# A three-stage transformer block: the last attention chunk's closing steps moved into the first steps of the second feed-forward

## The chip, the cores and the metric

The kernel runs on one core of one Trainium2 chip. The metric is the device time of one execution in microseconds (us), as the median of several runs. TensorE (PE) does matmuls and its own weight loads, VectorE (DVE), ScalarE (ACT) and GpSimd (POOL) work elementwise, and SyncE (SP) issues most DMAs. Each engine takes its own instructions in order and waits on semaphores.

## The reference

The input x has 8 sequences of 512 rows of 256 numbers, 4096 rows in all. Three stages follow one another, and each needs the whole output of the one before only through its own rows, except for the ranking of the rows by expert:

```
x = x + 0.5 * ffn(layernorm(x))
x = x + attention(layernorm(x))
x = x + 0.5 * ffn(layernorm(x))

def attention(x):                       # 16 heads of 16, causal, per sequence of 512
    q, k, v = x @ Wq.T, x @ Wk.T, x @ Wv.T
    out = softmax(mask(q k.T / 4)) @ v
    return out @ Wo.T

def ffn(x):                             # both feed-forwards have the same weights
    shared = (silu(x @ w1) * (x @ w2)) @ w3             # 1024 hidden
    scores = sigmoid(x @ router_w)                      # 16 experts
    top2 = the two largest of scores + bias
    routed = sum over the top2 e of scores[e] * swiglu_e(x)   # 256 hidden each
    return shared + routed
```

All is float32. The large products are made of three products of a high and a low part (a value and its rest after rounding), summed in PSUM.

## The kernel before

The program is a row of blocks, each of which ends when every engine has come to its end: a first norm, the first feed-forward (tiles named `f_`, the same function as the second), the attention (`at_`), and the second feed-forward (`f_` too). In the function `feed_forward` the second one is the case `exact`.

**The attention** works on 8 chunks c of 512 rows (a chunk is one sequence) and on 4 groups of 4 heads in each, so on 32 groups G; `TG` is 32. All engines run the same double loop, over rounds i and over 11 steps s of a round, and small tables say what stands at which (i, s). Round i makes the scores of group i+1 (`score1`, for the row maxima) and of group i (`score2`, then the exponentials on ACT), and at step 8 the product of group i-1 with the values (`weigh`, L2258). The groups of a chunk are followed, some rounds later, by its closing: the sums are turned over (`turn_over`, L2087), stored and fetched back broadcast over partitions (`send` L1807, `fetch` L1814), the product is scaled (L2092), multiplied with Wo (`project_out`, L2282), added to x (L2101), normed (L2039, L2045, POOL L1884 and L1886, L2128), turned (`turn2`, L2292 on PE, L2013 on ACT) and multiplied with the router weights (`route`, L2303, `logits` L2107). In rounds 32 to 37 there is no group left, and only the closing of chunks 6 and 7 is done. `shift` (L2065) negates a group's maxima; SP lays them down with L1789, and the group's `score2` waits for that DMA.

**The second feed-forward** has three parts. The shared part runs over 5 of 8 chunks and 8 slices j of the hidden size, 40 steps n = 8c + j (`BEHIND` is 5): PE multiplies slice n with w1 and w2 (`up`, L1408, 12 matmuls), then slice n-1 with w3 (`down`, L1424 and L1428, 12 matmuls). ACT makes silu (L1034) and the high part (L1038), DVE the product `f_hid` (L1250) and the low part (L1266). At j = 2 and 3 the next chunk's x is split (L984, L1087), at j = 0 the last chunk's result is added to x (L1213). Ahead of the first step the shared weights w1, w2, w3 are loaded in six pieces of 512 KB (SP L687) and split: high parts by ACT (L991), low parts of two by DVE (L1333) and of four by POOL (L916). The routing stands in the same steps: `routing(n)` on DVE finds the two best experts of all 4096 rows and the slot of each in a list sorted by expert, done in `slots` at n = 9 (L1149 to L1151); then POOL sends each row to its two slots in `rows_by_slot` with 64 indirect DMAs (`send`, L931), after loading rows in 16 pieces of 256 KB into four buffers (`load`, L922). From `INVERT_AT` = 13 on, eight times at every second step, DVE marks (`marks`) and PE inverts the list, which `homes` reads at n = 31. SP meanwhile loads the high parts of the 16 experts' weights, 768 KB each (`load_high`, L700), the last two after `homes`.

The routed part then runs over 80 blocks of 128 sorted rows. Its first block is fetched by SP (`fetch`, L735) when all 64 indirect DMAs have landed, and turned on PE (L1472) between `up` and `down` of the last shared step. Its weights' low parts come through a ring (L725). The last part does the remaining three chunks of the shared part and the sums.

## Time and profile before

| what | value |
|---|---|
| median of 3 runs | 1559.57 us (1558.65 to 1566.25) |
| the profiled execution's own time | 1568.19 us |
| its span, first to last instruction | 1566.0 us |
| mean granted TensorE clock | 0.968 of full |
| PE busy | 1466.1 us, 94% of the span |
| DVE, ACT, POOL busy | 960.9, 662.3, 594.4 us |

Times of rows count from the span's start. A row of the timeline has the start, the busy time, the engine and line, the operation with its tiles, how many instructions are merged (x), and in brackets how long the engine had been idle and what released it. The three runs differ by 7.6 us among themselves.

### The profile page before, as it was taken

How to read it: one execution, taken by the hardware profiler on the slowest of the kernel's cores; microseconds unless marked ns; L12 is line 12 of the kernel's file. 1: busy time of each engine (PE TensorE's matmuls, PEld its weight loads, DVE VectorE, ACT ScalarE, POOL GpSimd, SP SyncE). 2: the span in 40 equal slices, each digit the busy share in tenths (PEclk: the TensorE clock that was granted, in tenths of full speed). 3: DMA queues.
4: the chain of work that ended last, by engine and by line, in shares of the span. 5: the costliest groups of instructions: out<-in, count | busy, mean ns of one | idle time of the engine just before them, and what ended most of it. 6: DMA issues, size and time to landing. Idle time of an engine off the chain costs nothing. (4 is left out here: it accounts for less than half of the span.)

```text
span 1566.0 us, 29057 instructions
## 1 busy us (share of the span) xinstructions
PE 1466.1 (94%) x8999; PEld 1195.1 (76%) x9032; DVE 960.9 (61%) x2015; ACT 662.3 (42%) x1338; POOL 594.4 (38%) x836
## 2 busy tenths in 40 slices
PE   4999999999989979999999999948999999999998
PEld 4888888888878766667766666537888888888887
DVE  4678855555545657677677666316774455565566
ACT  2334444343433535665665566514322333443332
POOL 4618830233323023464466444403487033333100
PEclk9999999999999989999999999858999999999999
DMA  9696989535385953354555454224396344347841
GB/s 316 249 365 227 347 318 353 190 107 183 106 293 169 333 150 93 90 130 117 141 135 128 118 127 121 80 96 144 129 343 227 111 145 127 123 153 249 284 143 54
DMA packets 176804, 286.32 MB, mean 183 GB/s; under 512 B 20754, under 2 KB 125714, under 8 KB 176418
## 3 DMA queue, kind: packets, MB, share of 16 engines
q1 hardware_dynamic: 134914, 206.83, 41.8%
q0 software_dynamic: 19104, 56.64, 9.8%
q10 hardware_dynamic: 22656, 21.11, 4.6%
q8 instruction: 81, 1.33, 0.3%
q14 instruction: 49, 0.40, 0.1%
HBM read 144.20 MB, written 110.36 MB: 163 GB/s over the span
## 5 line engine op out<-in xcount | busy, mean ns | idle before, releaser
L1408 PE MATMUL f_bank<-f_xparts,f_sw 128*128 128x512 f32 x1536 | 382.0, 398 | 12.4 <-DVE f_sw L1333 9.2
L1408 PEld LDWEIGHTS f_bank<-f_xparts,f_sw 128*128 128x128 f32 x1536 | 287.3, 193 | 69.0 <-issue 12.2
L963 POOL DMA_INDIRECT outputs_by_choice<-f_yr,f_home x160 | 153.4, 959 | 394.5 <-DVE f_yr L1359 338.4
L2056 DVE TENSOR_REDUCE at_mx<-at_ps 128x1 f32<-128x384 f32 (+3 forms) x352 | 213.9, 632 | 111.9 <-PE at_ps L2188 104.7
L1963 ACT ACTIVATE at_pT<-at_ps 128x512 f32<-128x512 f32 (+1 forms) x352 | 194.4, 559 | 71.6 <-PE at_ps L2204 62.7
L1879 POOL TENSOR_SCALAR_AFFINE_SELECT at_pT<-at_pT 128x128 f32<-128x128 f32 (+2 forms) x352 | 124.2, 361 | 221.1 <-ACT at_pT L1963 216.7
L931 POOL DMA_INDIRECT rows_by_slot<-f_xq,slot x128 | 145.2, 1134 | 111.5 <-DVEq L1152 73.2
L1250 DVE TENSOR_TENSOR f_hid<-f_sil,f_bank 128x512 f32<-128x512 f32 x128 | 87.9, 687 | 145.1 <-PE f_bank L1408 104.8
L2204 PE MATMUL at_ps<-fa_qT,fa_kT 98*128 98x256 f32 (+3 forms) x512 | 172.4, 390 | 4.6 <-DMA fa_qT<-at_mT 2.5
L1348 DVE TENSOR_TENSOR f_sil<-f_sil,f_bank 128x256 f32<-128x256 f32 x160 | 67.4, 421 | 163.0 <-ACT f_sil L1056 160.0
L1038 ACT CAST f_hparts<-f_hid 128x512 fp32r<-128x512 f32 x128 | 79.4, 620 | 201.6 <-DVE f_hid L1250 185.3
L1424 PE MATMUL f_bank<-f_sw,f_hparts 128*128 128x256 f32 x1024 | 147.2, 287 | 9.3 <-ACT f_hparts L1038 8.4
L2184 PE MATMUL at_ps<-fa_kT,fa_qT 96*128 96x512 f32 (+2 forms) x384 | 146.6, 398 | 9.8 <-DMA fa_kT<-at_loT 7.8
L1424 PEld LDWEIGHTS f_bank<-f_sw,f_hparts 128*128 128x128 f32 x1024 | 139.3, 192 | 19.4 <-ACT f_hparts L1038 9.6
L1034 ACT ACTIVATE f_sil<-f_bank 128x512 f32<-128x512 f32 x128 | 76.4, 597 | 155.0 <-PE f_bank L1408 137.0
L1056 ACT ACTIVATE f_sil<-f_bank 128x256 f32<-128x256 f32 x160 | 61.6, 385 | 172.6 <-PE f_bank L1496 172.6
L1266 DVE TENSOR_TENSOR f_hparts<-f_hid,f_hparts 128x512 fp32r<-128x512 f32 x128 | 88.3, 690 | 41.7 <-ACT f_hparts L1038 37.7
L1496 PE MATMUL f_bank<-f_ring,f_hparts 128*128 x320 | 100.7, 396 | 7.1 <-SPq L730 7.1
L2204 PEld LDWEIGHTS at_ps<-fa_qT,fa_kT 98*128 98x128 f32 x512 | 90.1, 202 | 9.5 <-ACT at_pT L1963 5.5
L1064 ACT CAST f_hparts<-f_bank 128x256 fp32r<-128x256 f32 x160 | 59.7, 373 | 84.0 <-PE f_bank L1472 72.7
L1496 PE MATMUL f_bank<-fa_whi,f_hparts 128*128 x320 | 94.8, 418 | 0.0
L1496 PE MATMUL f_bank<-f_whi,f_hparts 128*128 x320 | 93.9, 415 | 0.1
(231 smaller groups left out, 2511.7 us busy)
## 6 DMA issues: line engine op xcount, KB each, us to landing
f_ring<-weights_in_parts SPq DMA_DIRECT2D x32, 768.0 KB
weights_in_parts<-fa_whi SPq DMA_DIRECT2D x30, 768.0 KB, 8.4
f_rawx<-rows_by_slot ACTq DMA_DIRECT2D x152, 128.0 KB
f_whi<-weights_in_parts SPq DMA_DIRECT2D x16, 768.0 KB
fa_ew<-in_L_ffn_routed_w_dram SPq DMA_DIRECT2D x42, 256.0 KB, 5.1
rows_by_slot<-zero POOLq DMA_DIRECT2D x10, 1024.0 KB, 22.1
f_xq<-xn_rows POOLq DMA_DIRECT2D x32, 256.0 KB
fa_ew<-outputs_by_choice SPq DMA_DIRECT2D x8, 1024.0 KB, 10.3
```

The lines of the kernel that those rows point to most:

```text
L931: nc.gpsimd.indirect_dma_start(dram.xs, bass.IndirectOffsetOnAxis(ap=g.slot[:, at:at + 1], axis=0), xq[:, h % 4, t, :], None).then_inc(sca ...
L963: nc.gpsimd.indirect_dma_start(dram.yk, bass.IndirectOffsetOnAxis(ap=home[:, i:i + 1], axis=0), yr[:, i % 4, :], None).then_inc(y_st[i % 4 ...
L1250: v.tensor_tensor(hid[:, j % 2], sil[:, j % 2, :], psB[j % 2][:, :], ALU.mult).then_inc(h_done, 1)
L1266: v.tensor_tensor(hparts[:, j % 2, 1], hid[:, j % 2], hparts[:, j % 2, 0], ALU.subtract).then_inc(h_lo, 1)
L1408: ins = pe.matmul(ps[j % 2][:, :], sw12[:, wp, k, w, j * P:(j + 1) * P], xparts[:, u, xp, k, :], start=(i == 0), stop=(i == 3 * KD - 1))
L1424: pe.matmul(psO[t], hparts[:, j % 2, 0, t * P:(t + 1) * P], sw3[:, wp, j, :], start=(j == 0 and wp == 0 and t % 2 == 0), stop=False, skip_ ...
L1496: ins = pe.matmul(rUp[r % 2][:, :], xsP[:, r % 2, xp, k * P:(k + 1) * P], w[:, bass.ds(base + k * 2 * RH, 2 * RH)], start=(n == 0), stop=( ...
L1879: p.affine_select(out=own, in_=own, compare_op=ALU.is_ge, fill=0.0, base=0, pattern=[[0, heads], [1, P]], channel_multiplier=-1).then_inc( ...
L1963: s_.activation(pT[:, i % SLOTS, 0:w], ps2[i % RING2][:, 0:w], ACT.Exp).then_inc(ex_done, 1)
L2056: v.tensor_reduce(own, ps1[i % RING1][:, 0:heads * w].rearrange("p (j a x) -> p j a x", a=min(heads, 2), x=w), AX.X, ALU.max).then_inc(mx_ ...
L2184: pe.matmul(ps[:, j * w:(j + each) * w], qT[0:ROWS, G % KEEP, (h + j) // 2, qi * P:w], kT[0:ROWS, G % KEEP, h + j:h + j + each, 0:w], star ...
L2204: ins = pe.matmul(ps[:, j * w:(j + 1) * w], kT[0:LAST_ROWS, G % KEEP, h + j, ki * P:(ki + 1) * P], qT[0:LAST_ROWS, G % KEEP, (h + j) // 2, ...
```

## The change

The attention's loop ends after round 33. The closing of chunk 7's second half, from the move of group 31's result to the router product, leaves the attention and stands in the first eight steps of the second feed-forward's shared part, in functions named `end` and `end_behind` on each engine. The attention hands its semaphores and tiles over in `tail`, and the memory of the two blocks is laid out so that both can be live. The loads and splits of the six shared weight pieces and of chunk 0's x go from the feed-forward's head into the attention's rounds 29 to 32 (`ASK` on SP, `HIGH` on ACT, `LOW` on DVE; POOL takes no part). The routing starts 8 steps later (`R0`), `slots` is at n = 16, the inversion at n = 18 to 34 and `homes` at n = 36. POOL loads 12 pieces of rows at once before it sends, and 4 more in between. The order in which SP loads the 16 experts is written out; experts 14 and 15 wait for `homes`, experts 0 to 2, whose place is taken by the pieces of rows, come last. The first norm and the first feed-forward are as before.

The core of the diff (what is left out hands over names, tiles and semaphores, and lays out memory):

```diff
+
+    ROUNDS = range(-4, TG + 2)
+
+
+    ASK = {(TG - 3, 4): (0, 1), (TG - 2, 4): (2, 3), (TG - 1, 4): (4, 5)}
+    HIGH = {(TG - 2, 3): 0, (TG - 2, 9): 1, (TG - 1, 3): 2, (TG - 1, 9): 3, (TG, 6): 4, (TG, 7): 5}
+    LOW = {(TG - 1, 1): 0, (TG - 1, 3): 1, (TG - 1, 7): 2, (TG, 1): 3, (TG, 7): 4, (TG, 8): 5}
...
@@ -1841,8 +2056,16 @@
                         fetch(*half_of(i))
                     if s == AT_PROJ and proj_of(i, s) is not None:
                         lay_out(proj_of(i, s))
-                    if s == AT_WEIGH + 2 and 0 <= i - 1 < TG:
+                    if s == AT_WEIGH + 2 and 0 <= i - 1 < TG - 1:
                         take_out(i - 1)
+                    if (i, s) in ASK:
+
+                        sp.wait_ge(*full("value", (NB_ - 1, CT - 1)))
+                        for piece in ASK[i, s]:
+                            sp.dma_start(PIECES[piece][0], piece_source(z, dram, piece)
+                                         ).then_inc(sw_in[piece // 2], 16)
+                        if (i, s) == (TG - 2, 4):
+                            sp.dma_start(raw0[:], dram.xnT[:, :, 0:CHUNK]).then_inc(x0_in, 16)
                     if gr == 1 and s == 10 and 0 <= c - 2 < NB_:
                         for k in range(KD):
...
+            def high_weights(piece):
+                raw, parts = PIECES[piece]
+
+                act.wait_ge(sw_in[piece // 2], 32)
+                s_.copy(parts[:, 0], raw).then_inc(sw_hi, 1)
 
...
+                    if (i, s) in HIGH:
+                        high_weights(HIGH[i, s])
+                    if (i, s) == (TG, 9):
+
+                        act.wait_ge(x0_in, 16)
+                        act.wait_ge(s2_done, TG * UN)
+                        s_.copy(own.xparts[:, 0, 0], raw0[:]).then_inc(x0_hi, 1)
...
-                    if gr == 3 and s == 0 and c == NB_:
-                        normalize2(c - 1)
+                    if (i, s) in LOW:
+                        raw, parts = PIECES[LOW[i, s]]
+                        dve.wait_ge(sw_hi, LOW[i, s] + 1)
+                        v.tensor_tensor(parts[:, 1], raw, parts[:, 0], ALU.subtract)
+                    if (i, s) == (TG, 9):
+                        dve.wait_ge(x0_hi, 1)
+                        v.tensor_tensor(own.xparts[:, 0, 1], raw0[:], own.xparts[:, 0, 0], ALU.subtract)
...
-                load_res(1, U(1))
-                load_x(1)
-            else:
...
+
+                sp.wait_ge(tail.o_ev, tail.TG)
+                sp.wait_ge(tail.scaled, 2 * tail.C)
+                sp.dma_start(tail.av[tail.HD:2 * tail.HD, 1, :], tail.oT[0:P:2, 1, :]).then_inc(tail.o_ld[1], 16)
+                sp.dma_start(tail.sums[tail.HG * 8:2 * tail.HG * 8, 1, :], tail.oT[1:P:2 * HEAD, 1, :]
+                             ).then_inc(tail.o_ld[1], 16)
+            load_x(1)
+            load_res(0, U(0))
...
+                sp.wait_ge(tail.rc, 2 * C + 2)
+                sp.dma_start(dram.rec[1].rearrange("h (x n) -> (h x) n", x=8), tail.turned[:, 1, :]
+                             ).then_inc(tail.rec_out, 16)
+                sp.wait_ge(tail.rec_out, 16 * (2 * C + 2))
+                sp.wait_ge(tail.scaled, 2 * C + 1)
+                sp.dma_start(tail.rec[:], dram.rec[1].rearrange("h (o n) -> h o n", o=1)
+                             .to_broadcast([HEADS // KD, HEAD, CHUNK])).then_inc(tail.rec_in, 16)
+
+                sp.wait_ge(tail.o_ld[1], 16 * tail.TAKEN * (tail.TG // 2))
+                for e in (7, 8, 9):
+                    load_high(e)
+                next_x(2)
+                sp.wait_ge(res_done, 2)
+                sp.dma_start(dram.x2[bass.ds(C * CHUNK, CHUNK), :].rearrange("(t p) d -> p t d", p=P), tail.xres[:]
+                             ).then_inc(tail.x2_st, 16)
+                sp.wait_ge(tail.normed2, C + 1)
+                sp.dma_start(dram.xn[bass.ds(C * CHUNK, CHUNK), :].rearrange("(t p) d -> p t d", p=P), tail.xn2[:]
+                             ).then_inc(tail.xn2_st, 16)
+                sp.wait_ge(t2_free, KD)
+                sp.dma_start(dram.xnT[:, :, bass.ds(C * CHUNK, CHUNK)], tail.xnT2[:]).then_inc(tail.xnT2_st, 16)
+                store(0, U(0))
+                next_res(2)
+
+                sp.wait_ge(routed, 1)
+                sp.wait_ge(tail.x2_st, 16 * NC)
+                sp.wait_ge(tail.xn2_st, 16 * NC)
+                sp.wait_ge(tail.xnT2_st, 16 * NC)
+                for e in (3, 4):
+                    load_high(e)
+                next_x(3)
+                for e in (5, 6):
+                    load_high(e)
+                store(1, U(1))
+                next_res(3)
+                next_x(4)
+                sp.wait_ge(weighed, 1)
+                for e in range(10, far_experts):
+                    load_high(e)
+                store(2, U(2))
+                next_res(4)
+                next_x(5)
+                store(3, U(3))
+                sp.wait_ge(homed, 1)
+                for e in range(far_experts, E):
+                    load_high(e)
+
+                for s in range(4):
+                    sp.wait_ge(scat[s], 16 * (CT // 2) * TOPK * 3)
+                for e in range(3):
+                    load_high(e)
             else:
                 for e in range(4):
                     load_expert(e)
...
             if fill:
                 for b0 in range(0, NB, 8):
@@ -942,13 +1051,26 @@
...
+                pool.wait_ge(tail.eps2, tail.C + 1)
+                nc.gpsimd.tensor_tensor(tail.rstd[:, 1, :], tail.veps[:, 1, :], g.mhalf[:, 0:CT], ALU.pow
+                                        ).then_inc(tail.rs2, 1)
             pool.wait_ge(placed, 1)
...
+            def scores():
+                nc.scalar.activation(score.rearrange("p t e -> p (t e)"), g.logits[:], ACT.Sigmoid).then_inc(scored, 1)
+
...
+            def end(n):
+
+
+                if n == 5:
+                    for k in range(KD):
+                        act.wait_ge(t2_full, k + 1)
+                        nc.scalar.copy(tail.xnT2[:, k, :], (psR, psC)[k][:]).then_inc(t2_free, 1)
+                elif n == 7:
+                    act.wait_ge(logit_in, 1)
+                    scores()
 
...
+            def end(n):
+
+                C = tail.C
+                if n == 0:
+                    for u in range(2):
+                        dve.wait_ge(tail.o_ld[u], 16 * tail.TAKEN * (tail.TG // 2))
+                    dve.wait_ge(tail.rec_out, 16 * 2 * C)
+                    v.reciprocal(tail.turned[:, 1, :], tail.sums[:, 1, :]).then_inc(tail.rc, 1)
+                elif n == 4:
+                    dve.wait_ge(tail.xr_ld, 16 * NC)
+                    for u in range(2):
+                        dve.wait_ge(out_full, u + 1)
+                        rows = tail.xres[:, 2 * u:2 * u + 2, :].rearrange("p t d -> p (t d)")
+                        v.tensor_tensor(rows, rows, (psR, psC)[u][:], ALU.add).then_inc(res_done, 1)
+                    dve.wait_ge(res_done, 2)
+                    dve.sem_inc(g.held, 1)
+                    for t in range(CT):
+                        v.bn_stats(tail.stat[:, 1, t, :], tail.xres[:, t, :]).then_inc(tail.st, 1)
+                    dve.wait_ge(tail.st, tail.counted + CT)
+                    dve.sem_inc(g.held, 1)
+                    for t in range(CT):
+                        ins = v.bn_aggr(tail.mv[:, 1, t, :], tail.stat[:, 1, t, :])
+                    ins.then_inc(tail.var2, 1)
+                elif n == 7:
+                    dve.wait_ge(routed, 1)
+                    v.tensor_copy(g.logits[:, C * (CT * E):(C + 1) * (CT * E)], psR[:, 0:CT * E]).then_inc(logit_in, 1)
+
+            def end_behind(n):
+
+                if n == 2:
+                    dve.wait_ge(tail.rec_in, 16 * (2 * tail.C + 2))
+                    v.tensor_tensor(tail.attnT[:, 1, :], tail.av[:, 1, :], tail.rec[:], ALU.mult).then_inc(tail.scaled, 1)
+                elif n == 4:
+                    dve.wait_ge(tail.rs2, tail.C + 1)
+                    dve.wait_ge(tail.xn2_st, 16 * tail.C)
+                    for t in range(CT):
+                        ins = v.tensor_scalar(tail.xn2[:, t, :], tail.xres[:, t, :], tail.mv[:, 1, t, 0:1],
+                                              tail.rstd[:, 1, t:t + 1], ALU.subtract, ALU.mult)
+                    ins.then_inc(tail.normed2, 1)
+
+            def routing_late(n):
+
+                if n < 8:
+                    routing(n)
+                elif n == 8:
+                    slots()
+                elif n == 9:
+                    block_experts()
+                elif n in (11, 13):
+                    k = (n - 11) // 2
+                    gates(k, (one1, one2)[k])
+                    if k == 1:
+                        words_out()
+                        dve.sem_inc(weighed, 1)
...
                         low_part(PART_AT.index(n), 0)
                     if j == 3 and not last:
                         low_x(1 - u, c + 1)
-                    if c < 2:
+                    if exact:
+                        end_behind(n)
+                        if 0 <= n - R0 < 16:
+                            routing_late(n - R0)
+                    elif c < 2:
...
+            def end(n):
+
+                if n == 3:
+                    pe.wait_ge(tail.scaled, 2 * tail.C + 2)
+                    for u in range(2):
+                        for j in range(2):
+                            t = 2 * u + j
+                            for k in range(KD):
+                                ins = pe.matmul((psR, psC)[u][:, j * z.D:(j + 1) * z.D],
+                                                tail.attnT[:, k, t * P:(t + 1) * P], tail.wo[:, k, :],
+                                                start=(j == 0 and k == 0), stop=(k == KD - 1), skip_group_check=True)
+                        ins.then_inc(out_full, 1)
+                elif n == 5:
+                    pe.wait_ge(tail.normed2, tail.C + 1)
+                    for k in range(KD):
+                        for t in range(CT):
+                            ins = pe.transpose((psR, psC)[k][:, t * P:(t + 1) * P], tail.xn2[:, t, k * P:(k + 1) * P],
+                                               g.ident[:, :])
+                        ins.then_inc(t2_full, 1)
+                elif n == 6:
+                    pe.wait_ge(t2_free, KD)
+                    for t in range(CT):
+                        for k in range(KD):
+                            ins = pe.matmul(psR[:, t * E:(t + 1) * E], tail.xnT2[:, k, t * P:(t + 1) * P], g.rw[:, k, :],
+                                            start=(k == 0), stop=(k == KD - 1))
+                    ins.then_inc(routed, 1)
+
...
 
-        PARTS, INVERT_AT = NT * TOPK // QN, 13
+        PARTS, INVERT_AT = NT * TOPK // QN, 18 if exact else 13
```

On PE the seam between the two blocks was this before (each row is a line, an operation, its tiles and its shape, in program order):

```order
L2292 MATMUL at_psX<-ident,at_xn 128x128 x8
L2303 MATMUL at_psX<-rw,at_xnT 128x16 x8
L2282 MATMUL at_psX<-at_wo,at_attnT 128x256 x8
L2292 MATMUL at_psX<-ident,at_xn 128x128 x8
L2303 MATMUL at_psX<-rw,at_xnT 128x16 x8
L1660 UNCONDITIONAL_BRANCH
L1370 UNCONDITIONAL_BRANCH
L1408 MATMUL f_bank<-f_xparts,f_sw 128x512 x24
L1424 MATMUL f_bank<-f_sw,f_hparts 128x256 x8
L1428 MATMUL f_bank<-f_sw,f_hparts 128x256 x4
```

and is this now, up to step 3 (L1592 is `up`, L1606 and L1610 are `down`, L1623 is the product with Wo):

```order
L2525 MATMUL at_psX<-ident,at_xn 128x128 x8
L2536 MATMUL at_psX<-rw,at_xnT 128x16 x8
L1876 UNCONDITIONAL_BRANCH
L1558 UNCONDITIONAL_BRANCH
L1592 MATMUL f_bank<-f_xparts,f_sw 128x512 x24
L1606 MATMUL f_bank<-f_sw,f_hparts 128x256 x8
L1610 MATMUL f_bank<-f_sw,f_hparts 128x256 x4
L1592 MATMUL f_bank<-f_xparts,f_sw 128x512 x12
L1606 MATMUL f_bank<-f_sw,f_hparts 128x256 x8
L1610 MATMUL f_bank<-f_sw,f_hparts 128x256 x4
L1592 MATMUL f_bank<-f_xparts,f_sw 128x512 x12
L1623 MATMUL f_bank<-at_wo,at_attnT 128x256 x8
```

The closing of chunk 7 moved from ahead of the branch, where nothing stood between its parts, to behind the `up` of steps 3, 5 and 6.

On DVE the attention ends now, from the last maxima of round 30 on, with this (L2301 is `shift` of group 31, L2388 the low parts of the weights, L2391 that of x, L1357 the first row of the next block):

```order
L2292 TENSOR_REDUCE at_mx<-at_ps_0 128x1
L2323 RECIPROCAL at_turned<-at_sums 64x64
L2388 TENSOR_TENSOR f_sw<-f_raw,f_sw 128x2x512
L2301 TENSOR_SCALAR at_mT<-at_psX 16x128
L2388 TENSOR_TENSOR f_sw<-f_raw,f_sw 128x2x512 x2
L2328 TENSOR_TENSOR at_attnT<-at_av,at_rec 128x512
L2388 TENSOR_TENSOR f_sw<-f_raw,f_sw 128x2x512
L2388 TENSOR_TENSOR f_sw<-f_raw,f_sw 128x1024 x2
L2391 TENSOR_TENSOR f_xparts<-at_raw,f_xparts 128x1024
L2343 COPY logits<-at_psX 128x64
L1876 UNCONDITIONAL_BRANCH
L1203 UNCONDITIONAL_BRANCH
```

One low part stands ahead of `shift`, where before `shift` came right behind the reciprocal.

On SP the end of the shared part was this (L700 the experts' high parts, L735 the first sorted rows, L725 the ring):

```order
L672 DMA f_rawx<-xn_turned 128x2x512
L700 DMA f_whi<-weights_in_parts 128x1536 x4
L681 DMA x_plus_shared<-f_xr 128x4x256
L735 DMA f_rawx<-rows_by_slot 128x256 x4
L725 DMA f_ring<-weights_in_parts 128x1536 x3
```

and is this now (L762, L797 and L787 are the same three):

```order
L738 DMA f_rawx<-xn_turned 128x2x512
L747 DMA x_plus_shared<-f_xr 128x4x256
L762 DMA at_whi<-weights_in_parts 128x1536 x5
L797 DMA f_rawx<-rows_by_slot 128x256 x4
L787 DMA f_ring<-weights_in_parts 128x1536 x3
```

Five expert loads that wait for `homes` stand right ahead of the first sorted rows; it was two of the four, and a store was between.

## Rows read from the trace of the kernel before

**Rows 1.** Busy time by stretch, engines in turn, then clock, DMA share, GB/s

```profile
996.00:1021.00 25.00, 21.19 (x122) 9.92 (x114) 4.31 (x13) 11.07 (x21) 12.66 (x26) 0.66 0.27 87
1021.00:1060.00 39.00, 15.71 (x69) 13.39 (x66) 8.89 (x21) 7.84 (x10) 1.23 (x2) 0.59 0.37 126
1056.00:1066.00 10.00, 6.17 (x16) 4.90 (x17) 3.68 (x3) 7.66 (x8) 4.80 (x3) 0.54 1.06 366
1060.00:1078.50 18.50, 15.39 (x60) 12.45 (x61) 10.18 (x13) 8.80 (x11) 12.88 (x8) 0.77 0.64 211
1078.50:1246.00 167.50, 161.84 (x935) 140.54 (x936) 102.51 (x172) 48.74 (x78) 80.18 (x76) 0.98 0.51 182
```

**Rows 2.** Timeline from the last product with the values to the second feed-forward

```profile
1016.68 4.41 PE L2258 MATMUL at_psO<-at_pT,at_va 128*32 128x512 f32 x32 [1.49 <-POOL at_pT L1879]
...
1022.93 2.34 PE L2303 MATMUL at_psX<-rw,at_xnT 128*128 128x16 f32 x16 [0.82 <-ACT at_xnT L2013]
...
1031.24 0.69 DVE L2092 TENSOR_TENSOR at_attnT<-at_av,at_rec 128x512 f32<-128x512 f32 x1 [5.71 <-DMA at_rec<-one_over_sums]
...
1032.08 6.58 PE L2282 MATMUL at_psX<-at_wo,at_attnT 128*128 128x256 f32 x16 [6.81 <-DVE at_attnT L2092]
...
1050.68 0.23 DVE L2107 COPY logits<-at_psX 128x64 f32<-128x64 f32 x1 [6.45 <-PE at_psX L2303]
```

**Rows 3.** Timeline of the second feed-forward's first steps

```profile
1051.19 1.28 ACT L986 ACT_TABLE_LOAD   x1 [4.26 <-PEq L1660]
...
1057.38 1.04 ACT L991 CAST f_sw<-f_ew 128x1024 fp32r<-128x1024 f32 x1 [0.48 <-DMA f_ew<-in_L_ffn_shared_w_dram]
...
1058.46 2.56 DVE L1333 TENSOR_TENSOR f_sw<-f_ew,f_sw 128x1024 fp32r<-128x1024 f32 x2 [0.30 <-ACT f_sw L991]
...
1059.83 8.26 PE L1408 MATMUL f_bank<-f_xparts,f_sw 128*128 128x512 f32 x24 [9.18 <-DVE f_sw L1333]
...
1078.55 2.91 PE L1408 MATMUL f_bank<-f_xparts,f_sw 128*128 128x512 f32 x12
...
1082.73 2.91 PE L1408 MATMUL f_bank<-f_xparts,f_sw 128*128 128x512 f32 x12
```

**Rows 4.** A store of xn_turned, issue to landing

```profile
DMA to landing us min/median/max: 3.1/3.2/4.7
```

**Rows 5.** The closing's PE work of chunks 5 and 6, full clock

```profile
978.41 0.60 PE L2292 MATMUL at_psX<-ident,at_xn 128*128 128x128 f32 x4
...
983.12 1.85 PE L2303 MATMUL at_psX<-rw,at_xnT 128*128 128x16 f32 x16
...
987.55 1.97 PE L2282 MATMUL at_psX<-at_wo,at_attnT 128*128 128x256 f32 x8
```

**Rows 6.** Timeline of round 31, where the maxima of group 31 go round

```profile
1001.18 0.22 DVE L2065 TENSOR_SCALAR at_mT<-at_psX 16x128 fp32r<-16x128 f32 x1
1001.23 1.09 ACT L1963 ACTIVATE at_pT<-at_ps 128x512 f32<-128x512 f32 x2 [0.55 <-PE at_ps L2204]
...
1003.41 1.22 PE L2204 MATMUL at_ps<-fa_qT,fa_kT 98*128 98x512 f32 x2 [0.41 <-DMA fa_qT<-at_mT]
```

**Rows 7.** POOL's timeline, first and last of 64 sends

```profile
1112.53 1.08 POOL L931 DMA_INDIRECT rows_by_slot<-f_xq,slot  x1 [38.45 <-DVEq L1152]
...
1211.77 0.96 POOL L931 DMA_INDIRECT rows_by_slot<-f_xq,slot  x1 [0.30 <-issue]
```

**Rows 8.** Timeline around steps 32 to 39 and the first sorted rows

```profile
1208.81 3.00 PE L1408 MATMUL f_bank<-f_xparts,f_sw 128*128 128x512 f32 x12
...
1215.01 0.69 DVE L1250 TENSOR_TENSOR f_hid<-f_sil,f_bank 128x512 f32<-128x512 f32 x1 [9.47 <-remote]
...
1224.77 2.91 PE L1408 MATMUL f_bank<-f_xparts,f_sw 128*128 128x512 f32 x12
...
1245.67 2.91 PE L1408 MATMUL f_bank<-f_xparts,f_sw 128*128 128x512 f32 x12
...
1249.85 0.38 PE L1472 MATMUL f_bank<-ident,f_rawx 128*128 128x128 f32 x2
```

249 lines of the change are left out of this document (139 added, 110 removed).

## The prediction

> **What bounds the kernel now.** I read the stretches first [rows 1]. In the shared part, from its step 3 on, PE is busy 161.8 of 167.5 us at a clock of 0.98: PE is the bound there. Between the last product with the values and the second feed-forward's first matmul it is busy 15.7 of 39 us at 0.59, and in the following 18.5 us it works at 0.77. So the seam is where time lies open. The timeline says why [rows 2]: PE's last full-width work ends at 1016.68 + 4.41 = 1021.09. Then one chain runs, in which each engine waits for the one before: the reciprocals go out and come back (DVE waits 5.71 us for that DMA), PE waits 6.81 us and multiplies with Wo, the rows are normed, turned and routed, and the last copy ends at 1050.91. Only then do the loads of the next block start, and its first matmul stands at 1059.83, released by a low part of the weights [rows 3]. Step 3 starts at 1078.55, the next step at 1082.73. The bound of the seam is thus a chain of latencies, 57.5 us from 1021.09 to step 3.
>
> **The change, part by part.** I cost the new seam from the same point, 1021.09, to a step 3 that has caught up with the moved work.
>
> 1. *To the end of the attention's block.* Chunk 6's closing stays. Its router product ends at 1022.93 + 2.34 = 1025.27 [rows 2]. On ACT the cast of x, 1.04 us by its like [rows 3], now stands ahead of the two copies that this product waits for, so it ends at 1026.3, but the block ends with the store of the turned rows: issued when the copies are done, at about 1024.1, it lands 3.2 us later [rows 4], at 1027.3. The next block began 0.3 us after the last copy (1050.91, then 1051.19) [rows 2, 3]; with as much again for PE's first weights the first matmul is at 1027.9. That is 6.8 us from 1021.09. The weight pieces need not be waited for, they were split in rounds 30 to 32.
>
> 2. *First matmul to step 3.* The first two `up` took 8.26 us, with the clock at 0.5 at first [rows 3]; the new ones start cold too, since PE has a hole of about 1.5 us ahead of them. Then a `down`, 4.18 - 2.91 = 1.27 us, and a full step, 4.18 us: 13.7 us. The stops between the first steps of before (POOL's low parts, and the 18.5 us in which three steps are done) go.
>
> 3. *The moved PE work*, at full clock: 2 x 1.97 for the product with Wo, 2 x 0.60 for the turn, 1.85 for the router [rows 5]: 7.0 us. It cannot hide, PE is the bound. Before it was paid cold (6.58 us for Wo alone).
>
> Sum: 6.8 + 13.7 + 7.0 = 27.5 us in place of 57.5, **30.0 us gained** if nothing waits. Four costs come off.
>
> 4. *The attention's last rounds: 3 us.* DVE now has a low part ahead of `shift` of group 31, 2.56/2 = 1.28 us by its like [rows 3]. Behind `shift` are the DMA of the maxima and `score2` of group 31, for which PE already waited 0.41 us [rows 6]: the whole 1.28 us arrives. ACT gets a cast of 1.04 us in each of four places where exponentials are due; PE can be two units ahead at most. ACT's own idle in round 31 (0.55 us before a pair of exponentials, [rows 6]) covers about half of each, in round 30 more: I take 1.7 us, bounds 0 and 4 x 1.04. The casts of pieces 4 and 5 stand where ACT waits for the last product anyway: nothing, unless they slip behind it, then 2.1 us. SP's new 3.5 MB lie in rounds 29 to 31 behind no waiting transfer of the same step; 0 to 3 us. Bounds of the term together: 1.3 and 8.
>
> 5. *The reciprocals of the last half: 2 us.* DVE takes the last reciprocal ahead of step 0's product and stops in step 2 until the broadcast is back, with its low part of step 2 behind it, which `down` of step 2 needs. Before, 10.15 us passed from the last product to that scaling (1021.09 to 1031.24): ACT's copy, the move, the reciprocal, out and back. The copy, some 0.6 us, stays in the attention; the rest starts with the block at about 1027.6 and ends at 1037 on an idle queue, while DVE comes to it at about 1041. But SP has put 1.5 MB on its queue ahead of it, and POOL issues 3 MB in the same moment. At the 366 GB/s of [rows 1] all 4.5 MB last 12.3 us from 1028.5, to 1041, and the store and the fetch come after that, some 5 us: 1046. The wait is 0 in the one case and 5 us in the other, minus what PE has in hand (its Wo product waits for the same row): 2 us, bounds 0 and 6. The rule in the Trainium skill, "DMA: Bandwidth & Descriptors", section on queues, rings and completion order, is that each DMA engine takes turns between the queues at packets, and it speaks for the middle: SP's 1.5 MB would share with an equal part of POOL's and be through after 3 MB, at about 1037, not 1041.
>
> 6. *ACT and DVE in steps 7, 8 and 16: 2.5 us.* The sigmoid now stands between silus, with a table load on either side, 1.28 us each [rows 3], and 0.6 us of its own: 3.2 us on an engine that has some 3 of 4.18 us free in a step. DVE has the residual (4 instructions) and the first routing step, or `slots`, together in steps 8 and 16, near 4 us ahead of the low part, where PE's order gives some 2.8 us. 0.5 + 1 + 1; bounds 0 and 5. The Trainium skill, "ScalarE: Activation LUTs", section on what ACT_TABLE_LOAD costs, puts a switch at about 2.66 us with its drain; by it the two switches would take 5.3 us and the stop in step 8 would be 2 us longer. The rows show 1.28.
>
> 7. *The seam to the sorted rows: 2 us.* `homes` is at n = 36 in place of 31, and five loads of 768 KB follow it on SP's queue, then the first rows, which PE turns between the parts of the last step, 4.18 us after the start of step 39 (1245.67 and 1249.85, [rows 8]). From `homes`, 5.5 us into step 36, there are 3 x 4.18 + 4.2 - 5.5 = 11.2 us; 3.9 MB take 10.7 us at 366 GB/s, plus a start of about 2. So 1.5 us late, and the ring's first load behind it: 2, bounds 0 and 6.
>
> Steps 18 to 34 with marks and inversions cost PE what 13 to 29 did. The scatter: `slots` moves to n = 16, which starts at about 1109 in the new order, so the first send is at about 1117 against 1112.5 [rows 7]. 64 sends took 100 us with 12 loads between; with 4 they take some 92: done at 1209, while the first sorted rows are wanted at about 1226. It is hidden, with 17 us to spare.
>
> Sum: 30.0 - 3 - 2 - 2.5 - 2 = **20.5 us**. There is one more open term. In step 32 DVE stood still 9.47 us for something that the trace calls remote, and step 33 and 34 came late: 1208.81 to 1224.77 is 16.0 us for two steps of 4.18 [rows 8], 7.6 us lost. It lies in the scatter and in code that the change only shifts. I leave it in; if it is gone the gain is 28, if a second one comes it is 13.
>
> The profiled execution would be 1568.19 - 20.5 = 1547.7 us. The median of the runs shown is 8.6 us below it, and I take the same difference: 1559.57 - 20.5 = **1539 us**.
>
> **The rivals.**
> *A, all of it hides:* terms 4 to 7 near their lower bounds, or the stop of step 32 is gone: 27 to 34 us, about 1529. For it: DVE and ACT have half of their time free in the shared part [rows 1]. Against: four engines now meet in steps 0 to 8.
> *B, the start is flooded:* the reciprocals come at 1046 or later because all of SP's and POOL's bytes are ahead, DVE, then PE stop in step 2 and again in step 4 or 5, where the stores and the norm hang on the same queues, and the clock falls to 0.5 again. A stop of 6 us and three steps at half clock (3 x 4.18) are 18 us in place of term 5's 2: the gain is 4.5 us, 1555. For it: the share was 1.06 of the DMA engines at the last start of this block [rows 1]. Partly so: 10 to 14 us gained, 1547.
> *C, the scatter sets the end of the shared part:* now at 64 sends in 100 us it ends 37 us before the first sorted rows are turned [rows 7, 8]. The rows would be turned at about 1228, so it decides from 1226 on, and the kernel gets slower only if the last send lands after 1250, so 133 us after the first one, 2.1 us a send. Sends at twice the price (3.1 us, 200 us for 64) would put the end at 1317 and the time at some 1627; at 2.2 us a send it would be 1567. Against: 3 MB of rows are loaded ahead, fewer loads stand between, and the expert loads are the same bytes. Little.
> *D, the attention pays:* exponentials late by each cast in full, the clock lower from round 30 on (it was 0.66 from 996 on, [rows 1]): 8 us and half of a 14 us round, 15 us in place of 3: gain 8.5, 1551.
>
> **How the numbers follow.** The forecast (gain 15 to 26) has 0.48, A 0.24, B and its part 0.13, D 0.08, something that loses in several small places but stays within 0.5% 0.03, C or another loss 0.04. The range has to cover A and the mild sides of B and D: 1527 to 1550. About 0.5%, 7.8 us, is what a measurement of this kernel can tell from no change: faster 0.91, same 0.05, slower 0.04.
>
> **What would show each step.** Right: PE's first matmul of the second feed-forward 7 to 10 us after the last product with the values, step 3's `up` within 25 us of it, a clock of 1.0 by step 2 and no fall after; DVE's scaling in step 2 waits less than 6 us; the scatter ends before step 39. Wrong: a long wait of DVE for the broadcast, PE waiting in rounds 30 and 31 for ACT, PE waiting for the first sorted rows or for the experts' weights by more than 6 us, or a stop called remote in another place. The gain would be wrong as a whole if the steps after step 3 became longer than 4.18 us on average by more than 0.1 us, since there are 36 of them.

## The result

The changed kernel took 1571.32 us (median of 20 runs, 1567.41 to 1577.61), the kernel before 1565.86 us beside it (20 runs, 1558.65 to 1572.06). The ratio is 1.0046, 95% interval 1.0031 to 1.0062: within 0.5% of no change, on its slow side. Forecast were 1539 and a range of 1527 to 1550. A later session, in which both kernels were measured again side by side, gave another answer: there the same kernel was faster than the kernel before by 0.7% (1546.8 against 1556.2 us; one of its seven runs took 3571.9 us, counts as slow and is outside the ratio). Both results have to be explained.

**The profile after.** The first stretches are better than before and the last is not. Windows of the changed kernel; columns as in [rows 1]:

```profile
1060.00:1187.00 127.00, 122.91 (x728) 106.53 (x727) 86.73 (x153) 39.93 (x62) 50.65 (x47) 1.00 0.43 150
1187.00:1220.00 33.00, 16.46 (x67) 11.79 (x65) 4.23 (x7) 1.81 (x3) 22.45 (x23) 0.65 0.27 96
1220.00:1250.00 30.00, 28.50 (x153) 24.41 (x153) 16.19 (x29) 8.77 (x14) 0.00 (x0) 0.93 0.31 114
```

The shared part runs at full clock with PE busy 97%, until 1187. Then, for 33 us, PE is busy half of the time at a clock of 0.65, DVE 13% and ACT 5%, with a DMA share of 0.27. Only GpSimd is at its usual pace, a send every 1.27 us. A timeline of PE in that stretch shows what "half busy" is:

```profile
1191.57 2.91 PE L1592 MATMUL f_bank<-f_xparts,f_sw 128*128 128x512 f32 x12
...
1199.33 0.60 PE L1606 MATMUL f_bank<-f_sw,f_hparts 128*128 128x256 f32 x2 [0.75 <-issue]
...
1204.28 0.37 PE L1606 MATMUL f_bank<-f_sw,f_hparts 128*128 128x256 f32 x1 [1.53 <-issue]
...
1209.91 0.37 PE L1610 MATMUL f_bank<-f_sw,f_hparts 128*128 128x256 f32 x1 [1.74 <-issue]
...
1214.81 0.58 PE L1592 MATMUL f_bank<-f_xparts,f_sw 128*128 128x512 f32 x1 [2.21 <-issue]
...
1219.71 3.63 PE L1592 MATMUL f_bank<-f_xparts,f_sw 128*128 128x512 f32 x7 [0.81 <-issue]
```

Matmuls that otherwise come in rows of 12 within 2.91 us come one to three at a time, with mostly 0.7 to 2.2 us between them, and the profile knows nothing that they wait for ("issue"). It shows no wait for data. Step 32 starts at 1191.57, step 34 at 1226.88: the two steps in it lasted 35.3 us, in place of the 10.8 of the same kernel where nothing crawls (e14 below, 1187.30 to 1198.09). I call it the crawl. The kernel before has one too, of 7.6 us, in step 32 [rows 8]; it is the "open term" of the prediction. On GpSimd the changed kernel differs in one thing: with twelve buffers its last load goes out at 1156.11, and then 44 sends follow each other; before, a load stood after every fourth send until 1196.73 and only 12 sends had none. (A half-chunk, h in the code, is 4 sends.)

The seam itself, timeline of the changed kernel:

```profile
1020.82 4.49 PE L2491 MATMUL at_psO<-at_pT,at_va 128*32 128x512 f32 x32 [1.49 <-POOL at_pT L2102]
...
1032.11 3.09 POOL L1026 DMA_DIRECT2D f_xq<-xn_rows  x4 [11.35 <-POOLq L1876]
1032.12 7.91 PE L1592 MATMUL f_bank<-f_xparts,f_sw 128*128 128x512 f32 x24 [2.16 <-DVEq L1523]
...
1035.18 5.79 POOL L1026 DMA_DIRECT2D at_ew<-xn_rows  x8
1036.17 0.50 SPq L811 DMA_DIRECT2D one_over_sums<-at_turned  x1
...
1049.27 0.63 SPq L815 DMA_DIRECT2D at_rec<-one_over_sums  x1
...
1053.24 0.69 DVE L1381 TENSOR_TENSOR at_attnT<-at_av,at_rec 128x512 f32<-128x512 f32 x1 [8.23 <-DMA at_rec<-one_over_sums]
...
1053.98 5.31 PE L1623 MATMUL f_bank<-at_wo,at_attnT 128*128 128x256 f32 x16 [5.59 <-DVE at_attnT L1381]
```

The first matmul comes 6.8 us after the last product with the values, as worked out. But the 16 KB of reciprocals, stored at 1036.17, could be fetched only at 1049.27: SP and GpSimd had filled the queues (DMA share over 1.00 from 1036 to 1047, 0.08 from 1048 to 1049.3). DVE waited 8.23 us, PE 5.59, and the product with Wo ran cold: the granted clock was 1.00 from 1041 to 1050, 0.55 from 1050 to 1054 and 0.73 from 1054 to 1060, and its 16 matmuls took 5.31 us, where they take 3.61 at a clock of 1.00 (e16 below).

### The profile page after: what moved, and what is told of

The parts are those of the page before. It is cut to its first block and busy times, and to the rows that moved or that the text cites. A ratio compares the mean times of both kernels' runs of the same rounds, so it can differ in the third digit from the quotient of the medians.

```text
span 1573.3 us, 29081 instructions
## 1 busy us (share of the span) xinstructions
PE 1466.4 (93%) x9032; PEld 1192.0 (76%) x9032; DVE 963.7 (61%) x2019; ACT 661.5 (42%) x1339; POOL 587.0 (37%) x832
## 5 line engine op out<-in xcount | busy, mean ns | idle before, releaser
L1592 PE MATMUL f_bank<-f_xparts,f_sw 128*128 128x512 f32 x1536 | 382.4, 398 | 10.5 <-issue 6.6
L1592 PEld LDWEIGHTS f_bank<-f_xparts,f_sw 128*128 128x128 f32 x1536 | 286.6, 193 | 69.4 <-issue 10.6
L2102 POOL TENSOR_SCALAR_AFFINE_SELECT at_pT<-at_pT 128x128 f32<-128x128 f32 (+2 forms) x352 | 127.7, 371 | 219.9 <-ACT at_pT L2186 215.7
L1606 PE MATMUL f_bank<-f_sw,f_hparts 128*128 128x256 f32 x1024 | 149.1, 288 | 11.0 <-issue 4.5
L1606 PEld LDWEIGHTS f_bank<-f_sw,f_hparts 128*128 128x128 f32 x1024 | 140.3, 193 | 22.1 <-ACT f_hparts L1169 8.7
L1040 POOL DMA_INDIRECT rows_by_slot<-f_xq,slot x96 | 108.1, 1126 | 125.4 <-DVEq L1285 96.8
L1610 PE MATMUL f_bank<-f_sw,f_hparts 128*128 128x256 f32 x512 | 84.9, 288 | 10.2 <-DVE f_hparts L1460 6.2
## 6 DMA issues: line engine op xcount, KB each, us to landing
rows_by_slot<-zero POOLq DMA_DIRECT2D x10, 1024.0 KB, 21.6
```

The source lines that it names most:

```text
L1040: nc.gpsimd.indirect_dma_start(dram.xs, bass.IndirectOffsetOnAxis(ap=g.slot[:, at:at + 1], axis=0), buffer(h)[:, t, :], None).then_inc(sca ...
L1592: ins = pe.matmul(ps[j % 2][:, :], sw12[:, wp, k, w, j * P:(j + 1) * P], xparts[:, u, xp, k, :], start=(i == 0), stop=(i == 3 * KD - 1))
L1606: pe.matmul(psO[t], hparts[:, j % 2, 0, t * P:(t + 1) * P], sw3[:, wp, j, :], start=(j == 0 and wp == 0 and t % 2 == 0), stop=False, skip_ ...
L2102: p.affine_select(out=own, in_=own, compare_op=ALU.is_ge, fill=0.0, base=0, pattern=[[0, heads], [1, P]], channel_multiplier=-1).then_inc( ...
```

## The experiments

Theory 1: the crawl comes from a long row of GpSimd's indirect sends with no other GpSimd work between them, and so from the twelve buffers, which are a side of the change that has nothing to do with the seam. Rivals: it comes with sends while the hardware queues carry nothing (theory 2), or it is an echo of the flood at the seam (theory 3). Ratios are to the kernel before on the same chip in the same session, with their 95% interval. Between two kernels I compare ratios.

**First session (kernel before 1566.0 us).**

e1, four buffers:

```diff
-                return more[:, h - 4] if exact and 4 <= h < 12 else xq[:, h % 4]
+                return xq[:, h % 4]
...
-            for h in range(12 if exact else 4):
+            for h in range(4):
...
-                        load(h + 11)
+                    load(h + 3)
```

> The changed kernel, with the second scatter's loads as in the kernel before: four buffers, the next load issued after each half-chunk's sends, so that 4 loads (1 MB) stand in the queue at its start in place of 12 (3 MB), and GpSimd's longest row of sends without a load is 12 or so sends at the end, as before (in the changed kernel no load follows 1156, and the sends go on to 1216). Theory 1 (a long row of GpSimd's indirect sends without a load between them is what stops PE, ACT and DVE in steps 32 to 34): the stop shrinks to the 7 to 8 us of the kernel before, the two slow steps of 18.1 and 17.3 us fall to 5 and 12, and the time is 15 to 20 us below the changed kernel's. Theory 2 (the stop comes with sends while the hardware queues carry nothing, which from 1174 on they don't in the changed kernel): the stop stays, and the time falls only by the start, where the 16 KB reciprocals no longer lie behind 3 MB, 4 to 6 us. Theory 3 (the loss is in the start's flood alone and the late steps wait for what it delays): 6 to 10 us less, with the rows of steps 32 to 34 only moved.

e2, rests until the sends have landed:

```diff
+                if exact and h >= 6:
+                    pool.wait_ge(scat[h % 4], per * (h // 4 + 1))
```

> The changed kernel, with GpSimd waiting after the sends of each half-chunk from the seventh on until these sends have landed, so that its row of sends has a rest every 16 us or so. Theory 1 (a long unbroken row of sends fills something that the other engines need, and a rest clears it): the gaps in PE's issue in steps 32 to 34 go or shrink to below 8 us, at the price of sends that end later, some 2 us for each half-chunk: 8 to 15 us below the changed kernel, unless the last send then lands after 1250, when the end pays. Theory 2 (sends without traffic of the hardware queues): the stop stays as long, and the time is the changed kernel's or up to 5 us above.

e3, the loads after the sums:

```diff
+            if exact:
+                pool.wait_ge(tail.rec_in, 16 * (2 * tail.C + 2))
             for h in range(12 if exact else 4):
```

> The changed kernel, with GpSimd's 12 loads of the second scatter issued only after the reciprocals' 16 KB have come back. What it measures is the flood at the seam (the second rival of the prediction): the fetch was issued 13.1 us after the store, DVE waited 8.23 us for it and PE 5.59 us for DVE, with the clock at 0.66. If that is the price of the start: step 4 falls from 15.1 to 9 to 10 us, and the time falls by 5 to 7 us, if nothing after it absorbs it. If the late stop in steps 32 to 34 is tied to the sends' end and not to PE's own place, then it absorbs this gain: what is won at step 4 is waited out at step 33, and the time falls by less than 2 us.

e4, filler on SyncE's queue:

```diff
                 next_x(5)
+                for i in range(14):
+                    sp.dma_start(dram.filler[i % 2], dram.xn[0:CHUNK // 2, :]).then_inc(fill_sem, 16)
+                    sp.wait_ge(fill_sem, 16 * (i + 1))
                 store(3, U(3))
```

> The changed kernel, with 14 copies of 256 KB in DRAM issued by SyncE one after the other in the stretch in which it was idle (1174 to 1222); they are work added and feed nothing. Theory 2 (sends while the hardware queues carry nothing let the engines' instruction stream stop): the stop in steps 32 to 34 shrinks to under 10 us and the time falls by 10 to 20 us. Theory 1 (a long row of sends without a load of GpSimd's own): the stop stays or grows, since the DMA engines have more to carry: the changed kernel's time or up to 10 us above.

Measured: e1 1547.2 us, ratio 0.9892 (0.9868 to 0.9917); e2 1568.8, 1.0017 (0.9999 to 1.0035); e3 1565.6, 0.9997 (0.9977 to 1.0018); e4 1576.9, 1.0091 (1.0058 to 1.0124). The windows 1180 to 1220 of e1, e2, e3 and e4, in this order:

```profile
1180.00:1220.00 40.00, 38.73 (x228) 33.67 (x227) 21.11 (x36) 10.95 (x18) 32.13 (x30) 1.00 0.53 183
```
```profile
1180.00:1220.00 40.00, 38.73 (x236) 33.73 (x234) 23.69 (x39) 11.31 (x18) 21.73 (x20) 1.00 0.26 93
```
```profile
1180.00:1220.00 40.00, 20.91 (x83) 14.75 (x83) 10.94 (x19) 3.65 (x6) 22.95 (x23) 0.64 0.26 92
```
```profile
1180.00:1220.00 40.00, 22.65 (x109) 16.90 (x108) 7.26 (x11) 3.65 (x6) 28.25 (x29) 0.77 0.60 181
```

PE's column is to be read: 38.7 us of 40 in e1 and e2, 20.9 and 22.7 in e3 and e4. Theory 2 falls: e4 doubled the DMA share and kept the crawl, and e2 has none at a share of 0.26. Theory 3 falls with e3, where the start is repaired and the crawl is there. e2 gained little, 0.3% by the ratios, because its last send began at 1243.67 and PE waited 16.44 us for the sorted rows (10.03 us busy from 1240 to 1260): the rests were dear, not useless. My price for them, 2 us a half-chunk, was too low. e1 gained more than I had forecast, 24 us by the ratios in place of 15 to 20, since its second feed-forward has no crawl at all. e3 was 0.49% below the changed kernel's ratio (of another session), 7.7 us; that the crawl would swallow this gain was wrong too.

**Second session (kernel before 1566.4 us).** e6 puts the one suspect into the kernel before:

```diff
                     pool.wait_ge(scat[(h - 1) % 4], per * ((h - 1) // 4 + 1))
-                    load(h + 3)
+                    if not exact or h + 3 < 8:
+                        load(h + 3)
```

> The kernel before, with GpSimd's loads of the second scatter ended after the eighth half-chunk: its later sends send old rows (so the rows that the experts get are wrong; no instruction but these 8 loads is left out). It puts the changed kernel's one suspect, a row of 44 sends without a load, into the kernel before, with nothing else of the change. Theory 1 (such a row stops PE, ACT and DVE in its last 25 to 30 us): the sends end some 9 us earlier, PE's busy time in the last 30 us before their end falls under half, and the time is 10 to 20 us above the kernel's before, 1576 to 1586. Rival (the stop comes from something else in the changed kernel, its x parts, its twelve buffers, the bytes at the seam): no longer stop than the 7.6 us of before, and 1560 to 1566, since the sends end earlier.

e5, e8 and e9 are e3 with something between the sends: e5 a plain transfer of 16 KB (the 32 KB of its expectation is wrong) after every 4 (first diff), e9 an operation of GpSimd's own after every 8 (second diff), e8 the same without `h % 2 == 0`, so after every 4. (No kernel has the number e7 or e13.)

```diff
+                if exact and 5 <= h < NH - 1:
+                    pool.dma_start(dram.small[h], dram.xn[h * 16:(h + 1) * 16, :]).then_inc(small_in, 16)
```
```diff
+                if exact and 5 <= h < NH - 1 and h % 2 == 0:
+                    nc.gpsimd.tensor_tensor(g.rest[:, h, :], g.eps[:, 0:CT], g.mhalf[:, 0:CT], ALU.pow).then_inc(paused, 1)
```

> The kernel with the loads after the sums (e3, 1565.6), with one plain transfer of 16 rows in DRAM (32 KB) put on GpSimd's queue after the sends of each half-chunk from the sixth to the fifteenth; it is work added. GpSimd does not wait for them until all sends are out. If what clears the stop in e1 is a plain transfer in GpSimd's queue between the sends: the steps 31 to 39 take 4.2 to 5 us as in e1, the last send goes out near 1219, and the time is that of e1 within 4 us, 1543 to 1551. If only a real rest (e2 waited until the sends had landed) or e1's smaller flood cleared it: the stop stays and the time is 1560 to 1570.

> As e5, but with an operation of GpSimd on 128x4 elements that takes 1.04 us (the same as its L1059) in place of the transfer: a rest in the row of sends with nothing put in the queue. If a microsecond's rest after every 4 sends is enough: 1543 to 1551, as e5 is to be. If a transfer between them is what counts: e5 fast and this one 1560 to 1570. If neither is fast, the number of buffers is what told e1 from the changed kernel.

> As e8, with the rest after every 8 sends and not every 4 (5 rests). If a rest clears the stop and what fills up takes 9 sends or more to do so (in the kernel before the stop began after about 9 sends without a load), this is as fast as e8 or up to 5 us faster, since the sends end 5 us earlier and in e1 the wait for the sorted rows at the end was for them. If the stop builds up over fewer sends than 8: 5 to 15 us above e8.

Measured: e6 1587.2 us, ratio 1.0126 (1.0091 to 1.0160); e5 1544.2, 0.9860 (0.9830 to 0.9890); e8 1547.6, 0.9874 (0.9847 to 0.9901); e9 1544.5, 0.9861 (0.9832 to 0.9890). Windows of e6, then of e9:

```profile
1180.00:1220.00 40.00, 21.30 (x66) 14.07 (x66) 10.80 (x18) 3.90 (x7) 21.89 (x22) 0.57 0.28 96
```
```profile
1180.00:1220.00 40.00, 35.40 (x208) 30.55 (x206) 18.32 (x32) 10.69 (x17) 26.70 (x25) 1.00 0.52 189
```

So leaving out eight loads, nothing else, made the kernel before 20 us slower (1587.2, forecast were up to 1586) and gave it the changed kernel's crawl: PE's busy time and clock are near those of e3, 21.3 us at 0.57. And one microsecond of other work of GpSimd's after 8 sends takes it away: e9 is 21 us below e3 by the ratios (0.9997 - 0.9861). The 4.6 us that e9 lacks in that window are a gap of 1.27 us, which e1, e2 and e14 have too (38.73 of 40), and 3.3 us of its wait for the sorted rows, which it reaches sooner. GpSimd's timeline of e9 shows a rest:

```profile
1181.74 1.04 POOL L1078 TENSOR_TENSOR rest<-eps,mhalf 128x4 f32<-128x4 f32 x1
1182.98 1.04 POOL L1041 DMA_INDIRECT rows_by_slot<-at_ew,slot  x1 [0.20 <-issue]
```

The operation ends at 1182.78 and the next send starts 0.20 us later: the row of sends stands still for 1.24 us, and that is all.

e3 and e9 belong to two sessions, so it must be shown that there was a crawl to clear in e9's. The first feed-forward, which no experiment of the first two sessions touches, shows it: its own 64 sends end at 214, with 12 at the end without a load, and there PE stops in e9 too. Windows of e9, then of e14 (fourth session, no crawl):

```profile
195.00:235.00 40.00, 36.97 (x201) 31.14 (x201) 23.46 (x38) 18.18 (x28) 15.19 (x16) 0.96 0.89 316
```
```profile
195.00:235.00 40.00, 40.00 (x232) 35.04 (x231) 26.05 (x41) 20.47 (x32) 15.82 (x15) 1.00 0.97 364
```

One step of the first feed-forward took 8.65 to 9.24 us in all ten profiles of the first two sessions and of the comparison above, which cost 4.8 to 7.1 us with its neighbours. In the ten profiles of the other three sessions no step there took over 5.8. So e2, e5, e8 and e9 crawl in the first feed-forward, where their sends are as before, and not in the second, where a rest, a wait or a transfer stands between them, within one execution. So does e1, though there both rows end alike, with 12 sends without a load.

**Third session (kernel before 1556.7 us).** e10 is the changed kernel with e9's rests but without e3's wait; e11 (first diff) the kernel before with two rests near the end of the sends of both feed-forwards; e12 (second diff) is e9 with an addition (0.20 us) for the power:

```diff
+                if NH - 3 <= h < NH - 1:
+                    nc.gpsimd.tensor_tensor(g.rest[:, h, :], g.eps[:, 0:CT], g.mhalf[:, 0:CT], ALU.pow).then_inc(paused, 1)
```
```diff
-                    nc.gpsimd.tensor_tensor(g.rest[:, h, :], g.eps[:, 0:CT], g.mhalf[:, 0:CT], ALU.pow).then_inc(paused, 1)
+                    nc.gpsimd.tensor_tensor(g.rest[:, h, :], g.eps[:, 0:CT], g.mhalf[:, 0:CT], ALU.add).then_inc(paused, 1)
```

> The changed kernel with the rest of 1.04 us after every 8 sends alone (e9 without its wait for the reciprocals). With the stop gone, what the flood at the seam costs can no more be waited out in it: step 4's 15 us in place of 7.6 should now show in the time. If so: 5 to 8 us above e9's 1544.5, 1550 to 1553, and 18 to 22 below the changed kernel. If the seam's loss is absorbed elsewhere: 1544 to 1547.

> The kernel before, with a rest of 1.04 us after the 8th and 4th last sends of both feed-forwards, of which nothing else is changed. The stop that the prediction left in (7.6 us in step 32 of the kernel before, after a row of 12 sends without a load) is the same thing as the changed kernel's if this takes it away: 6 to 9 us below the kernel before in the second feed-forward and 0 to 2 in the first, 1556 to 1560. If the 7.6 us have another cause: within 2 us of 1566.

> e9 with an addition in place of the power in each rest: 0.20 us (as its L1056) and not 1.04. If it is the length of the rest that clears what fills up, this is slower than e9 by 5 to 25 us. If any operation of GpSimd's own between the sends does it, however short: e9's time within 2 us, or 2 to 4 below it, since the sends end 4 us earlier.

Measured: e10 1547.6 us, ratio 0.9934 (0.9910 to 0.9958); e11 1555.9, 0.9997 (0.9982 to 1.0012); e12 1539.3, 0.9874 (0.9854 to 0.9894). e11 fits no theory as it stands: its profile has no crawl, and it is no faster. Also the kernel before was 10 us faster in the third session than in those before it. Hence the next session.

**Fourth session (kernel before 1556.2 us): both kernels once more, unaltered, each with a profile.**

> The changed kernel once more, unaltered, with a profile, on the same chip as the three below. If the stop comes on every chip: PE busy for under half of the last 25 us of the sends, and 0.3 to 0.6% above the kernel before. If it is a property of the chip that this call gets: where the kernel before takes about 1557, PE is busy through to the sends' end and the changed kernel is 14 to 20 us below it; where it takes about 1566, the stop is there again.

> The kernel before, unaltered, as a kernel of its own, so that it has a profile from this chip. Ratio to itself 1.000, within 0.2%. What is asked is whether its 7.6 us stop in step 32 is there (PE busy for about 5.3 of the 10 us from 1210): if it is, and e17 is as slow as this, the rests cost elsewhere what they bring; if it is not, e17 had nothing to clear.

> The kernel of e12 once more (an operation of 0.20 us after every 8 sends, and the loads after the sums). If operations of GpSimd's own between sends clear the stop wherever it is: 20 to 24 us below the kernel before on a chip where that takes 1566, 17 to 20 below on one where it takes 1557. If a short one does not, and e12 was fast only for want of a stop on its chip: on a chip with the stop it is as slow as e3, 0 to 5 us below the kernel before.

> The kernel of e11 once more (the kernel before with two rests of 1.04 us near the end of the sends). On a chip where the kernel before shows its stop: 6 to 10 us below it. On one where it shows none: within 2 us of it.

Measured: e14 (the changed kernel) 1546.8 us, ratio 0.9932 (0.9907 to 0.9957); e15 (before) 1557.1, 1.0007 (0.9989 to 1.0025); e16 1536.4, 0.9875 (0.9852 to 0.9899); e17 1556.3, 1.0001 (0.9987 to 1.0014). Windows of e14, then of e15:

```profile
1180.00:1220.00 40.00, 38.73 (x234) 33.68 (x233) 21.43 (x36) 11.51 (x19) 26.73 (x26) 1.00 0.43 151
```
```profile
1180.00:1220.00 40.00, 40.00 (x236) 35.00 (x235) 20.44 (x34) 12.05 (x20) 20.09 (x19) 1.00 0.53 183
```

The same two programs, and no crawl in either. The crawl needs a row of sends without a rest and something in which the sessions differ. That this is the chip, as the expectations put it, is not shown: the record numbers the chips of the five sessions 5, 3, 1, 5 and 6, and of the two with number 5 the first had the crawl and the fourth had none. Where it is absent, the changed kernel is 10.6 us faster (0.68% of 1556.2, interval 6.7 to 14.5), not the 14 to 20 that I expected of e14.

**Fifth session (kernel before 1556.4 us)**, to find e10 to e12 one with the crawl:

> The kernel of e12 and e16 (0.20 us of another operation after every 8 sends, loads after the sums). On a chip where the kernel before takes 1566: if a short operation clears the stop, 1538 to 1544, ratio 0.982 to 0.986; if it takes a microsecond's rest, the stop is back and the time is 1556 to 1566. On a chip where it takes 1556: 1536 to 1540 and nothing told.

> The kernel of e11 and e17 (the kernel before, two rests near the end of the sends). On a chip where the kernel before takes 1566: if its 7.6 us are the same stop, 1556 to 1559, ratio 0.993 to 0.996; if not, 1564 to 1568. On a chip where it takes 1556: ratio 1.000.

> The kernel of e10 (the changed kernel with rests of 1.04 us after every 8 sends and nothing else). On a chip where the kernel before takes 1566: 1546 to 1552, which beside the changed kernel's 1571 is what the stop costs it, 20 to 25 us. On a chip where it takes 1556: 1546 to 1549 as before.

Measured: e18 1539.1 us, ratio 0.9883 (0.9860 to 0.9905); e19 1555.8, 0.9997 (0.9983 to 1.0010); e20 1549.8, 0.9950 (0.9933 to 0.9967). It had none either. Three things stay open: whether a rest of 0.20 us clears the crawl where there is one (e9's microsecond does), whether two rests bring the kernel before from 1566 to 1556 us, and what the sessions differ in.

**What the parts cost.** e14, e15 and e16 ran on one chip. Timeline of e15, then of e14, then of e16: the attention's first product with its late wait, the last product with the values, and the first send of an expert's outputs.

```profile
582.40 0.77 PE L2184 MATMUL at_ps<-fa_kT,fa_qT 96*128 96x256 f32 x2 [8.56 <-DMA fa_kT<-at_loT]
...
1009.04 4.50 PE L2258 MATMUL at_psO<-at_pT,at_va 128*32 128x512 f32 x32 [1.49 <-POOL at_pT L1879]
...
1244.10 0.97 POOL L963 DMA_INDIRECT outputs_by_choice<-f_yr,f_home  x1 [39.13 <-DVE f_yr L1359]
```
```profile
585.35 0.77 PE L2417 MATMUL at_ps<-fa_kT,fa_qT 96*128 96x256 f32 x2 [8.26 <-DMA fa_kT<-at_loT]
...
1014.96 4.50 PE L2491 MATMUL at_psO<-at_pT,at_va 128*32 128x512 f32 x32 [1.49 <-POOL at_pT L2102]
...
1236.02 0.97 POOL L1085 DMA_INDIRECT outputs_by_choice<-f_yr,f_home  x1 [21.67 <-DVE f_yr L1547]
```
```profile
584.87 0.76 PE L2423 MATMUL at_ps<-fa_kT,fa_qT 96*128 96x256 f32 x2 [7.66 <-DMA fa_kT<-at_loT]
...
1014.43 4.50 PE L2497 MATMUL at_psO<-at_pT,at_va 128*32 128x512 f32 x32 [1.48 <-POOL at_pT L2108]
...
1227.85 0.97 POOL L1090 DMA_INDIRECT outputs_by_choice<-f_yr,f_home  x1 [21.63 <-DVE f_yr L1552]
```

From the last product with the values to the first expert's output: 235.06 us before, 221.06 changed (14.0 gained), 213.42 in e16 (21.6 gained). From the attention's first product to its last: 426.64, 429.61, 429.56, so 3.0 and 2.9 lost. The two together, 11.0 and 18.7 us gained, are near what the ratios of the session give, 10.6 and 19.5. The first product itself stands 3.0 and 2.5 us later than in e15, but this is within the spread of single profiles: it begins at 582.40 to 592.42 in the six profiles of the kernel before and its variants and at 583.93 to 593.06 in the fourteen of the changed kernel and its variants, and in the third and fifth sessions it is sooner in the changed ones.

The start of step 9 tells the seam from what comes behind it. Rows of e15, then of e16:

```profile
1096.59 2.91 PE L1408 MATMUL f_bank<-f_xparts,f_sw 128*128 128x512 f32 x12
```
```profile
1070.23 2.91 PE L1597 MATMUL f_bank<-f_xparts,f_sw 128*128 128x512 f32 x12
```

From the end of the last product with the values that is 83.05 us before and 51.30 in e16, 31.8 gained; in e14 it is 60.38, in the first profile of the changed kernel 58.82. Behind step 9, e16 stops five times in `down`, at steps 9, 12, 17, 25 and 33, and then waits for the sorted rows:

```profile
1074.96 0.74 PE L1615 MATMUL f_bank<-f_sw,f_hparts 128*128 128x256 f32 x4 [0.87 <-DVE f_hparts L1465]
...
1088.22 0.74 PE L1615 MATMUL f_bank<-f_sw,f_hparts 128*128 128x256 f32 x4 [0.47 <-DVE f_hparts L1465]
...
1111.31 0.74 PE L1615 MATMUL f_bank<-f_sw,f_hparts 128*128 128x256 f32 x4 [1.48 <-DVE f_hparts L1465]
...
1149.35 0.74 PE L1615 MATMUL f_bank<-f_sw,f_hparts 128*128 128x256 f32 x4 [1.27 <-DVE f_hparts L1465]
...
1187.89 0.74 PE L1615 MATMUL f_bank<-f_sw,f_hparts 128*128 128x256 f32 x4 [1.33 <-DVE f_hparts L1465]
...
1217.05 0.41 PE L1688 MATMUL f_bank<-ident,f_rawx 128*128 128x128 f32 x2 [2.32 <-DMA f_rawx<-rows_by_slot]
```

e16's gain over e14 is the flood at the seam. Its timeline there:

```profile
1034.05 0.64 SPq L816 DMA_DIRECT2D at_rec<-one_over_sums  x1
...
1037.95 3.07 POOL L1027 DMA_DIRECT2D f_xq<-xn_rows  x4 [23.57 <-DMA at_rec<-one_over_sums]
1038.47 0.68 DVE L1386 TENSOR_TENSOR at_attnT<-at_av,at_rec 128x512 f32<-128x512 f32 x1
...
1041.78 3.61 PE L1628 MATMUL f_bank<-at_wo,at_attnT 128*128 128x256 f32 x16
```

The store lands after 5.4 us in place of 13.1, nobody waits, and the product with Wo follows warm. e20 and e10 (rests, no wait for the reciprocals) stand at 0.9950 and 0.9934 like e14, e18 and e12 at 0.9883 and 0.9874 like e16: where there is no crawl the rests bring nothing, and the order of the loads brings 0.57 to 0.67%, 9 to 10 us.

## Why the prediction was wrong

**The mechanism of the seam was right.** Term by term, in the prediction's own order:
- *The base.* The forecast went from 1559.57 us, the median of three runs. Twenty runs of the kernel before gave 1565.86, so 6.3 us of the miss lie there. With this base the forecast is 1545.4, and the miss is 26 us.
- *1 and 2, end of the block and first steps:* 6.8 us to the first matmul; measured 6.8, in the changed kernel (1025.31 to 1032.12), in e14 and in e16. Step 3 was to start 20.5 us after the last product with the values; it started 20.2 after it (1045.48), in e16 20.1.
- *3, the moved work, 7.0 us:* 6.1 in e16 (31.2 us from step 3 to step 9, less six steps of 4.18). So without a wait the seam gained 31.8 us, 30.0 were forecast.
- *4, the attention's last rounds, 3 us:* right (its upper bounds add up to 10.5, not to 8); the attention got 2.9 and 3.0 us longer in e16 and e14, 1.5 in the first pair.
- *5, the reciprocals, 2 us (0 to 6): mis-sized.* By e3, e10 to e12, e14 and e16 it costs 8 to 10 us in the time, and 7.5 and 9.1 us at step 9 in the changed kernel's two profiles. I had the reciprocals back at 1037 or at 1046; on that clock, which is 4.2 us behind the changed kernel's, they were back at 1049. The store and the fetch behind the bytes took the 5 us allowed, but the queues ran full until 1048 (1044 on that clock, 1041 forecast). Without GpSimd's bytes, in e16, the store took 5.4 us and the fetch up to 3.9. The forecast also drew on the rule of "DMA: Bandwidth & Descriptors" in the Trainium skill, section on queues, rings and completion order, that each DMA engine takes turns between the queues, for a share of one half and so for SP's 1.5 MB through at about 1037. Here the store behind them landed no sooner than if all bytes of both queues had gone first; what shares the queues got is not shown. Then PE waited, and its clock fell. This is the mild part of rival B, and the forecast should have been near its middle.
- *6, ACT and DVE, 2.5 us (0 to 5): mis-sized.* The two table loads and the sigmoid took 3.24 us in e16 (1066.25 to 1069.49), as worked out from the rows. But PE stops five times for DVE's low part, 0.9, 0.5, 1.5, 1.3 and 1.3 us, 5.4 in all, where the kernel before has one such stop of 0.5 (e15). Four follow DVE's work of steps 8, 16, 24 and 32; I had looked at 7, 8 and 16 alone.
- *7, the sorted rows, 2 us:* 0.8 us of PE's wait in the changed kernel, 1.9 in e14, 2.3 in e16; right.

**The step that failed** is the last one of the sum: "It lies in the scatter and in code that the change only shifts. I leave it in". The change does not only shift it. The twelve buffers turn a row of 12 sends without a load into one of 44, and with the row the crawl in steps 32 and 33 grew from 7.6 us to 24.5 (35.3 in place of 10.8). I had the row under rival C and even counted the fewer loads as a point in favour ("fewer loads stand between"), since I asked of the scatter only when it ends. It ended at 1216, long before the rows were wanted, as C's bound said; it did its harm on the way. Of the prediction's signs of being wrong one was seen, DVE's long wait for the broadcast (8.23 us). For the stops called remote it looked to another place, and they came in the same one, longer.

**The sum with the right sizes.** Without the crawl 20.5 us were forecast. The changed kernel gained 10.6, since it pays the flood; half of the forecast is missing there with no crawl at all. e16 gained 19.5 (0.9875), which looks like the forecast and is in part luck: it is another kernel, in which term 5 is nothing, the seam is 1.8 us better and term 6 is twice as dear. With the crawl: 1571.3 - 1546.8 = 24.5 us on the changed kernel, 1565.9 - 1556.2 = 9.7 on the kernel before, which turns 9.4 us gained into 5.5 lost. These two differences are between sessions, and both include the crawl of the first feed-forward, 5.6 us in the profile before and 6.8 in the one after. They are less than the profiles give (24.5 and 7.6 us in the second feed-forward alone), and by how much single profiles differ from the median is seen above, so they are sizes and no balance. Within one session the same is shown by e6 (20 us for the eight loads left out); e3 against e9 gives 21 us for the rests, by the ratios of two sessions with the crawl.

**A kernel that beats both:** the changed one with the loads behind the reciprocals and a rest after 8 sends. e9 does it with the crawl about (1.39% below the kernel before, interval 1.10 to 1.68), e16 and e18 without (1.25 and 1.17%). e12's short rest is only known to do no harm.

## What to carry to other kernels

A stop that the profile puts down to "issue" or "remote" is a term with a cause, and not a constant: ask what stands in that stretch on every engine, the unhurried ones too, and whether the change lengthens it. Fewer instructions on an engine that is off the path can cost more than they save; a long row of indirect sends is broken up by a transfer or a microsecond of other work. A small transfer that a chain needs goes out before megabytes that nobody waits for yet, on all queues, because it may land only with the bytes in flight: the 16 KB here took 13.1 us behind and beside 4.5 MB, and 5.4 behind 1.5. And one profile, or one session, need not hold for the next.

## What the runs showed of the hardware

- In 44 indirect sends of GpSimd in a row (1.27 us each, DMA share 0.27) PE issued a matmul or two at a time, every 0.7 to 2.2 us, and DVE and ACT hardly anything (7 and 3 instructions in the 33 us from 1187, ACT idle for 21.1 us at once); GpSimd itself kept its pace. With 12 in a row 7.6 us were lost in the kernel before in the second feed-forward and 5.6 in the first; in e1, with as many, none in the second and 4.8 in the first, so the length of the row does not decide alone. A 16 KB transfer after every 4 sends or 1.04 us of arithmetic after every 8 prevented it. The waits for landed sends that stand between the sends in the changed kernel did not: GpSimd was idle for 0.30 us ahead of them, as ahead of every send. What fills up, if anything does, is not shown. The Trainium skill, "SBUF — State Buffer", section on the two separate sides, in its warning that DVE blocks GpSimd's DMA, describes the reverse case, in which GpSimd's sends are held up; no run here shows that.
- It came in three sessions of six, in all profiles of kernels with a long row and in every first feed-forward, and in no profile of the other three, with the same programs (kernel before 1566 against 1556 us). What tells the sessions apart is open. So a profile of one session need not hold for the next: here it decided the sign of the change.
- Two ACT table loads with a sigmoid between them took 3.24 us in e16: 1.28 us a load, and no gap around them.
